# A four-layer network on one core: layers 1 and 2 with three images in flight, and the scan's first states moved from TensorE to ScalarE

## The reference

```
h_new = exp(dt * A) * h_prev + dt * B * x
y     = sum over the 16 states of h_new * C
```

## Time and profile before

| what | us |
|---|---|
| median of 3 runs | 5764.54 (5763.57 to 5771.34) |
| profiled execution, its own time | 5764.76 |
| its span, first to last instruction | 5763.0 |
| start to the first scan | 129 |
| layer 0 with its scans | 129 to 3424 |
| layer 1 of image 0 alone, with the end of layer 0 | 3424 to 3673.8 |
| rounds 0, 1, 2, 3 of layers 1 and 2 | 277.6, 300.6, 289.8, 131.6 |
| layer 3 | 4673.4 to 5763.0 |

### The profile page before, as it was taken

The page is one execution under the profiler, slowest core; times in us unless marked ns, Lnnn a source line. Parts: engine busy times, 40 slices in busy tenths (PEclk is TensorE's granted clock), DMA queues, the critical chain, the costliest instruction groups (busy, mean ns, idle before and its releaser), DMA issues. The chain is left out here.

```text
span 5763.0 us, 81471 instructions
## 1 busy us (share of the span) xinstructions
PE 5022.4 (87%) x30948; PEld 4080.8 (71%) x30948; DVE 4308.4 (75%) x4771; ACT 2958.0 (51%) x5242; POOL 2869.7 (50%) x3500
## 2 busy tenths in 40 slices
PE   4898999998989989999899877778878879999999
PEld 2776777776777767777777753565656669999998
DVE  1999999999999999999999986484847553333333
ACT  3766677766677766666666633131313223333332
POOL 3776777776776776777777634362535310000000
PEclk8999999999999999999999987788888889999999
DMA  2000000000000010000000011002020010010100
GB/s 72 1 16 27 9 9 9 9 23 20 9 9 9 16 31 13 9 9 9 9 9 9 5 40 60 20 25 74 25 74 13 28 54 25 25 34 25 34 25 21
DMA packets 88530, 136.93 MB, mean 24 GB/s; under 512 B 5284, under 2 KB 85184, under 8 KB 88140
## 3 DMA queue, kind: packets, MB, share of 16 engines
q1 hardware_dynamic: 88140, 131.72, 7.0%
HBM read 89.23 MB, written 42.47 MB: 23 GB/s over the span
## 5 line engine op out<-in xcount | busy, mean ns | idle before, releaser
L730 DVE TENSOR_TENSOR_SCAN a_h<-a_dA,pw 128x770 f32<-128x770 f32 x1152 | 2012.5, 1747 | 130.0 <-PE pw L448 128.8
L595 ACT ACTIVATE a_dA<-a_dt,a_Aneg 128x384 f32<-128x384 f32 x2304 | 1314.5, 607 | 185.6 <-DVE a_h L730 176.4
L869 POOL TENSOR_SCALAR a_dBT<-a_dtxT,a_BC 128x768 f32<-128x768 f32 x1152 | 1024.6, 906 | 448.6 <-PE pw L448 345.6
L458 PEld LDWEIGHTS pw<-g_ident,a_h 128*128 128x128 f32 x6912 | 796.2, 142 | 491.8 <-DVE a_acc L750 197.6
L458 PE MATMUL pw<-g_ident,a_h 128*128 128x128 f32 x6912 | 968.4, 277 | 157.7 <-DVE a_acc L750 121.6
L750 DVE SCALAR_TENSOR_TENSOR a_acc<-pw,a_BC,a_acc 128x768 f32<-128x768 f32 x960 | 960.7, 1001 | 84.3 <-PE pw L458 56.7
L447 PE MATMUL pw<-g_ident,a_dBT 128*128 128x128 f32 x6912 | 948.1, 274 | 4.8 <-POOL a_dBT L869 4.8
L447 PEld LDWEIGHTS pw<-g_ident,a_dBT 128*128 128x128 f32 x6912 | 795.5, 141 | 6.5 <-POOL a_dBT L869 5.4
L1829 DVE TENSOR_TENSOR d_hf<-d_hf,ps 128x384 f32<-128x384 f32 x288 | 159.0, 554 | 560.7 <-ACT d_hf L1759 553.5
L821 POOL TENSOR_TENSOR a_xin<-a_xin,a_tm 128x384 f32<-128x384 f32 x432 | 432.9, 1002 | 32.7 <-ACT a_tm L517 7.7
L406 PE MATMUL ps<-a_xn,a_WinT 128*128 128x384 f32 x864 | 365.6, 525 | 30.7 <-ACT a_sz L573 15.1
(11 more groups left out here) (243 smaller groups left out, 9666.0 us busy)
## 6 DMA issues: line engine op xcount, KB each, us to landing
b_xs<-x SPq DMA_DIRECT2D x36, 576.0 KB, 5.0
a_xs<-in_x SPq DMA_DIRECT2D x24, 576.0 KB, 3.9
x<-a_xs SPq DMA_DIRECT2D x24, 576.0 KB, 3.0
b_x<-x SPq DMA_DIRECT2D x24, 576.0 KB, 4.4
e_xs<-x SPq DMA_DIRECT2D x24, 576.0 KB, 3.9
out<-e_xs SPq DMA_DIRECT2D x24, 576.0 KB, 3.0
a_sx<-in_x SPq DMA_DIRECT2D x54, 192.0 KB, 2.4
x<-b_x SPq DMA_DIRECT2D x16, 576.0 KB, 3.1
```

Of the source, the lines that this page charges most:

```text
L458: t = e.transpose(m["pw2"][:, c * 128:(c + 1) * 128], m[f"a_h{g % 2}"][:, c, 1 + tb * 128:1 + (tb + 1) * 128], ident[:])
L595: e.activation(m[f"a_dA{idx // 2 % NDA}"][:, idx % 2, 1:T + 1], m[f"a_dt{k % 2}"][:, c, :], ACT.Exp, scale=m["a_Aneg"][:, c, n:n + 1]).the ...
L730: e.tensor_tensor_scan(m[f"a_h{g % 2}"][:, c:c + 2, :].rearrange("p c t -> p (c t)"), m[f"a_dA{pi % NDA}"][:].rearrange("p c t -> p (c t)" ...
L869: t = e.tensor_scalar(m[f"a_dBT{g % 2}"][:, tb, :], m[f"a_dtxT{o}"][:, tb, :], m[f"a_BC{o}"][:, tb, n:n + 1], 1.0, ALU.mult, ALU.mult)
```

## The change

**Layer 0, first states.** The small matmul L448 is gone. A pair's PSUM columns are laid out as 771 elements: a constant 0, group one, a constant 1, a constant 0, group two (the three constants are written once, at the start, by VectorE). Column 0 of `a_dA` holds the first state of group one, the column under the constant 1 holds a decay of 0, and the next holds the first state of group two; the scan starts from 1.0, so that 1.0 times the state plus 0 is the state. ScalarE copies the two states from `a_st` into `a_dA` with one small instruction behind each pair's second exponential. `pe_b` moves to the last transpose, GpSimd's `kept` waits for ScalarE (`a_exp`) where it waited for TensorE, and `a_exp` counts three per pair.

**Layer 0, lent sums.** `LENT` has 7 entries, with 26 and 43 added.

**Layers 1 and 2.** `mix` is split into tasks with due times of their own: tokens, each convolution part, gelu and gate, outputs. Ahead of round 0 stand the end of layer 0 (its due times scaled by 0.35, so that it runs in with the tokens of image 0), all of layer 1 of image 0, and for image 1 the tokens and convolution part 0. Round b then has the rest of image b+1 (parts 1 and 2, all outputs, `head`) and, for image b+2, statistics, tokens and part 0. `head` is due at units 32 to 53 where it was at 49 to 53. The banks of PSUM are dealt out anew: token images have one bank where they had two, the outputs, statistics and gate logits share one bank (`sums_bank`, under one `Turn`), and the pixels' two banks are used by nothing else. The image `b_ti` is written under waits for the part of the convolution that still reads it. The DMA queue loads the rows for image b+3's statistics in round b.

```
-LENT = (20, 22, 24, 38, 41)
+LENT = (20, 22, 24, 26, 38, 41, 43)
...
-        if q > 0:
-            w.wait_ge("p_st", g - NS + 1)
-        first = m["a_st"][:, c:c + 2, p // 3] if q > 0 else m["a_zero"][:]
         for h in range(2):
             for tb in range(TB):
-                at = COL + h * (T + 1) + 1 + tb * 128
-                e.transpose(ps[:, at:at + 128], ...)
-        e.matmul(ps[:, COL:COL + T + 2:T + 1], ident[:], first, start=True, stop=True, skip_group_check=True).then_inc(s["pe_b"], 1)
+                at = COL + 1 + h * (T + 2) + tb * 128
+                t = e.transpose(ps[:, at:at + 128], ...)
+        t.then_inc(s["pe_b"], 1)
...
+            if c % 2:
+                if k % NQ > 0:
+                    w.wait_ge("p_st", g - NS + 1)
+                w.wait_ge("p_const", 4)
+                e.activation(dA[:, 0:T + 3:T + 2], m["a_st"][:, c - 1:c + 1, n] if k % NQ > 0 else m["a_zero"][:], ACT.Copy).then_inc(s["a_exp"], 1)
...
-        w.wait_ge("a_exp", 2 * pi + 2)
+        w.wait_ge("a_exp", 3 * pi + 3)
+        e.tensor_tensor_scan(m[f"a_h{g % 2}"][:, p % 3, :], m[f"a_dA{pi % NDA}"][:], m[f"pw{pi % 2}"][:, COL:COL + PAIR], 1.0, ALU.mult, ALU.add)...
...
+def win_at(b, n):
+    if b == 0:
+        return 5 + 1.2 * n
+    if b == 1:
+        return 31 + 1.9 * min(n, 11) + 0.9 * max(0, n - 11)
+    return 4 + 2.4 * n
+def conv_at(b, g, k):
+    if b == 0:
+        return 18 + 11.2 * g + 1.2 * k
+    if g == 0:
+        return (52.5 if b == 1 else 44.5) + k
+    return 1.5 + 11.5 * (g - 1) + 1.15 * k
+def out_at(b, g, i):
+    at, gap = (((31, 0.9), (42.2, 0.9), (53.4, 0.5)) if b == 0 else ((7.8, 0.6), (14.2, 0.9), (25.8, 0.8)))[g]
+    return at + gap * i
...
+def held(g):
+    return (0, 1, 1, 2, 2, 2)[g]
...
 def l12_dve(e, m, w):
-    march([post_dve(e, m, w, NCH - 1), norm_dve(e, m, w, 0, 0)], 0)
-    march([mix_dve(e, m, w, 0), matrices_dve(e, m, w), norm_dve(e, m, w, 1, 30)], 0)
-    march([head_dve(e, m, w, 0)], 0)
+    march([early(post_dve(e, m, w, NCH - 1), POST), pieces_dve(e, m, w, 0, 0.1, 0.3), norm_dve(e, m, w, 0, 2.6), tokens_dve(e, m, w, 0), matrices_dve(e, m, w),
+           conv_dve(e, m, w, 0, 0), conv_dve(e, m, w, 0, 1), conv_dve(e, m, w, 0, 2), gated_dve(e, m, w, 0), outputs_dve(e, m, w, 0),
+           pieces_dve(e, m, w, 1, 24, 0.7), norm_dve(e, m, w, 1, 29.2), tokens_dve(e, m, w, 1), conv_dve(e, m, w, 1, 0), head_dve(e, m, w, 0, 57.2, 61),
+           pieces_dve(e, m, w, 2, 55, 1)], 0)
     for b in range(NB):
-        side = [tail_dve(e, m, w, b - 1)] if b > 0 else []
-        side += [mix_dve(e, m, w, b + 1), head_dve(e, m, w, b + 1)] if b + 1 < NB else [weights3_dve(e, m, w)]
+        side = [tail_dve(e, m, w, b - 1)] if b > 0 else []
         if b + 2 < NB:
-            side.append(norm_dve(e, m, w, b + 2, NORM_AT))
+            side += [norm_dve(e, m, w, b + 2, 2), tokens_dve(e, m, w, b + 2), conv_dve(e, m, w, b + 2, 0)]
+        if b + 3 < NB:
+            side.append(pieces_dve(e, m, w, b + 3, 42, 1.9))
+        if b + 1 < NB:
+            side += [conv_dve(e, m, w, b + 1, 1), conv_dve(e, m, w, b + 1, 2), gated_dve(e, m, w, b + 1), outputs_dve(e, m, w, b + 1),
+                     head_dve(e, m, w, b + 1, 32.2, 51.5)]
         march(side, UNITS, lambda u: sparse_dve(e, m, w, b, u))
```

More of the change, by code:

```diff
@@ L1174, in mix_act @@
         e.activation(m["b_feff"][:], F1[:, 0:C], ACT.Copy).then_inc(s["a_f"], 1)
[L1176 to L1178 removed]
+    for n in range(NT + 2):
+        if n < NT:
+            yield win_at(b, n) + 0.5
             u = NT * b + n
@@ L1213, in gelu @@
-    def gelu():
-        for g in range(3):
-            v = m[f"b_cv{g % 2}"]
-            yield out_at(g, 0) - 3.4
-            w.wait_ge("v_c", 54 * b + 18 * (g + 1))
-            e.activation(v[:, 0, :], v[:, 0, :], ACT.Gelu).then_inc(s["a_g"], 1)
-            yield out_at(g, 0) - 2.9
-            w.wait_ge("p_c2", 24 * b + 8 * (g + 1))
-            w.wait_ge("p_g", 3 * b + g + 1)
-            e.activation(v[64:128, 1, :], v[0:64, 2, :], ACT.Gelu).then_inc(s["a_g"], 1)
-    yield from woven(tokens(), image(), products(), gelu())
+            w.wait_ge("v_c", 54 * (b - 1) + 18 * (held(r) + 1))
@@ L1367, in woven, with tokens_dve @@
-def woven(*gens):
-    side = [Paced(g) for g in gens]
-    while any(p.at is not None for p in side):
-        at = min(p.at for p in side if p.at is not None)
-        yield at
-        for p in side:
-            if p.at is not None and p.at <= at:
-                p.at = next(p.gen, None)
-                break
+def tokens_dve(e, m, w, b):
+    for n in range(NT):
+        yield win_at(b, n + 1) + 0.6
+        u = NT * b + n
+        w.wait_ge("pe_fw", u + 1)
+        w.wait_ge("a_f", 1)
+        w.wait_ge("pe_iv", u - 1)
+        e.tensor_tensor(m[f"b_tf{u % 2}"][:], token_banks(m)[1][:, 0:C], m["b_feff"][:], ALU.mult).then_inc(m.s["v_tf"], 1)
@@ new lines, in gated_dve, with outputs_dve @@
+def gated_dve(e, m, w, b):
+    for g in range(3):
+        v = m[f"b_cv{(3 * b + g) % 2}"]
+        yield out_at(b, g, 0) - 2
+        w.wait_ge("a_g", 6 * b + 2 * g + 2)
+        e.tensor_tensor(v[64:128, 1, :], v[64:128, 1, :], v[64:128, 2, :], ALU.mult).then_inc(m.s["v_g1"], 1)
+def outputs_dve(e, m, w, b):
+    s, x = m.s, m[f"b_x{b % 2}"]
+    for i in range(NT):
+        r, o = divmod(i, 3)
+        yield out_at(b, *divmod(i, 6)) + 0.3
+        w.wait_ge("pe_wo", NT * b + i + 1)
+        w.wait_ge("p_na", NT * (b + 1))
+        w.wait_ge(f"d_x{b % 2}{r}", 16 * (b // 2 + 1))
+        e.tensor_tensor(x[:, o, rows(r)], x[:, o, rows(r)], sums_bank(m)[:, 0:T], ALU.add).then_inc(s["v_y"], 1)
+        yield out_at(b, *divmod(i, 6)) + 0.55
+        w.wait_ge("v_y", NT * b + i + 1)
+        w.wait_ge("pe_gn2", b)
+        e.bn_stats(m["b_bn1"][:, o, r, :], x[:, o, rows(r)]).then_inc(s["v_b2"], 1)
@@ L1530, in mix_pool @@
-    yield from woven(normal(), sums(), gated())
+    for r in range(NQ):
+        yield win_at(b, 0) - 0.8 if r == 0 else win_at(b, 3 * r - 2)
+        src, sem, value = strip(m, b, r, 1)
+        w.wait_ge(sem, value)
+        w.wait_ge("v_b1", GN * (b + 1))
+        w.wait_ge("pe_t1", NT * b + 3 * (r - 1))
+        for c in range(CT):
+            e.tensor_scalar(m[f"b_xa{r % 2}"][:, c, :].rearrange("p (j h w) -> p j h w", j=3, w=16), patches(src[:, c]),
+                            sc[:, 0, c:c + 1], sc[:, 1, c:c + 1], ALU.mult, ALU.add).then_inc(s["p_na"], 1)
```

482 lines of the change are left out of this document (244 added, 238 removed).

## The result

| | us |
|---|---|
| kernel after, median of 4 runs | 5616.18 (5612.2 to 5624.31) |
| kernel before, beside it, median of 4 | 5767.94 (5763.57 to 5776.34) |
| ratio | 0.9737, 95% interval 0.972 to 0.9754 |
| profiled execution after, its own time and its span | 5612.2, 5610.3 |

What follows compares the result with a forecast made beforehand. VectorE was taken to set the pace in layer 0, with no engine full in layers 1 and 2 except in pieces. 5764.8 us less 79 (layer 0) and 135 (layers 1 and 2) gave 5551 us, range 5440 to 5660.

Steps and rivals of the forecast that it cites:

- ten named waits at 0.22 ... I take 3.0 us a chunk: Layer 0, first states: less VectorE waiting for TensorE wins 3.0 us a chunk, ends 0 and 8.0.
- 5 x 0.2 = 1.0 us lost a chunk: Layer 0: about five ScalarE copies ahead of `a_ob` delay the others by 1.0 us a chunk, ends 0 and 3.0.
- rival C: Layer 0: TensorE idles more and its clock falls; 20% at the low level would cancel both gains, 214 us; chance 0.05.
- 1.3 us a chunk: Layer 0, two more lent sums: VectorE's relief of 1.8 us, less chain delays, wins 1.3 a chunk, ends 0.6 and 1.8.
- chunks of about 133 us: Layer 0: a sign that the forecast is right, chunks of about 133 us where one undisturbed chunk took 136.4.
- Ahead of round 0: Layers 1 and 2, first stage: 183 us of VectorE work at 75% fill takes 244 us, against 249.8 before.
- some 3 us: Outputs sharing one bank: TensorE's wait for VectorE's addition is covered at 0.6 to 0.9 units apart, some 3 us.
- Rounds 0 and 1: Layers 1 and 2: earlier `head` shortens the rounds' end, winning 20 us (to 258) and 25 us (to 276).
- Round 2: Layers 1 and 2: 53 us less for tokens, 25 for `head`, 7 for taps, so 205 us from 289.8.
- the 7 us credited for taps: Round 2: 7 us less for taps that nothing covers.
- A: Layer 0: ScalarE takes TensorE's place, giving 5630 us; sign, TensorE waits for `a_ob` or `a_tm` beyond 3 us a chunk; chance 0.13.
- B: Layers 1 and 2: VectorE and GpSimd collide, mean tap rises to 1.9 us, giving 5637 us; chance 0.14.

Runs made afterwards that it cites:

- e3: The changed kernel with the five lent sums of before (20, 22, 24, 38, 41), so without 26 and 43; 0.9741 of the kernel before.
- e6: The changed kernel with TensorE's x projection in layer 0 due later (48.3 + j instead of 47 + 1.2 j); 0.9704 of the kernel before.
- e5: The changed kernel with only lent sum 26 taken back; 0.9708 of the kernel before, 17 us less than the change.
- e8: The changed kernel with the later x projection, two output banks ahead of round 0, and lent sum 26 replaced by 35; 0.9656 of the kernel before.
- e9: The changed kernel with the later x projection, two output banks ahead of round 0, and six lent sums (no 26, no 35); 0.9654 of the kernel before.
- e11: The changed kernel leaving out 36 of 54 input matmuls of layer 1 for image 0 (incomplete computation); 0.9718 of the kernel before.
- e4: The changed kernel with image 0's outputs ahead of round 0 alternating between two PSUM banks; 0.9714 of the kernel before.
- e7: The changed kernel with `head` late again, at units 49 to 52; 0.9808 of the kernel before, 41 us more than the change.
- e1: The kernel before with only layer 0's part of the change, layers 1 and 2 as before; 0.9835, 5677.4 us.

## Why the prediction came out as it did

**Layer 0, first states: right in kind, too small.** The step "ten named waits at 0.22 ... I take 3.0 us a chunk" gave 5.0 (e3, in chunks that keep the clock, with the copies already in it). The named waits undercounted. Pairs 10 to 13 and 17 went from 2.83 to 2.60 us each, and most of pairs 37 to 44 by 0.1 to 0.4: wherever TensorE has a projection at its side, it set the period, and the 0.22 us of the earlier trace rows came back whole. Such pairs don't show as long waits, but as a period above the 1.66 + 0.91 us of the earlier trace rows.

**The copies ahead of `a_ob`: right place, half the delay, other mechanism.** "5 x 0.2 = 1.0 us lost a chunk" was drawn as plain delay. The term is too large, since a copy takes 0.09 us of ScalarE's queue and not 0.2: the wait for `a_ob` grew by 0.46 us, from 2.15 to 2.61. And the delay is not passed on. Pair 23 in a chunk that keeps its clock is 4.09 us, where it was 4.19: nothing is lost. The cost comes through rival C in miniature: in ten of the 19 chunks with this wait the clock falls, 1.65 us each (132.95 against 131.3), 17 us in all. e6 takes it away. That the longer wait is what brings the falls is borne out by the counts (none in 19 chunks at 2.15 us in the kernel before, 7 to 16 in 19 at 2.61 us in each of seven runs, none in the 19 at 0.4 us in e6); why one chunk falls and the next does not is open.

**Two lent sums: the sum failed.** "1.3 us a chunk" was 0.2 (131.3 against e3's 131.4): 43 gives its 0.87 in full, and 26 loses 0.7 (e5), because its product stands in ScalarE's queue behind the softplus pieces. The prediction had named that place and still priced it positive. 35 lost 0.5 us a chunk in e8 (130.7 against e9's 130.2).

**The chunk of 133 us: luck.** The prediction's sign "chunks of about 133 us" came true in the ten chunks that lose the clock. Most of the others take 131.3: the states gave more than their term, the lent sums less, and what brings the chunk back to 133 is a fall of the clock that the forecast had not summed.

**Ahead of round 0: the step that failed most, 244 forecast, 273.** It divided all of VectorE's work by a fill of 75%. VectorE's busy time was forecast at 183 us and is 169 (8 us of this because the 64 taps took 1330 ns in the mean, not 1457), which by the same division would be 19 us less; the fill was 62%. The 68.7 us ahead of the first convolution hold 23.0 us of VectorE's work; at 75% these would take 31 us, so 38 us are missing from the forecast. There the end of layer 0 and the tokens of image 0 run through TensorE, and little for VectorE is ready (e11). The 204.4 us behind them have a fill of 71%, which is another 10 us over 75%, and the single output bank cost 12 us there (e4). 38 + 10 - 19 are the 29 us by which 273 passes 244. The prediction had this wait as what could eat the gain and put it down as covered at "some 3 us" between outputs; with taps of 1 to 2.6 us in front of the addition it is not.

**Rounds 0 and 1: mis-sized, 20 and 25 forecast, 8 and 13 measured.** (Round 0 of the order before varies from 273.9 to 279.9 us, so its 8 may be 5 to 10.) "What they win is the end" is right, and e7 gives 10 and 12 for it. The mistake was to take GpSimd's 28.9 and 15.4 us as time that all would win. The freed stretch fills with taps moved there until VectorE is full.

**Round 2: 205 forecast, 227.** 14 of the 22 us are the same step (25 credited for `head`, e7 gives 11; over the three rounds 70 were credited and 33 came, so it alone is some 37 us). The rest I can't assign, and the 7 us credited for taps stood on no row: this round takes 227 or, more often, 234 us by its clock, and the profiled run of the change is one of the short ones.

**Rivals.** A is refuted as a whole (the chunk did fall by 3.5 to 5.1 us), but it holds for 26 and 35, and its sign did show: TensorE's waits for `a_ob` and `a_tm` in chunk 10 went from 2.1 to 3.6 us, past the 3 that the prediction set. B is refuted: mean taps fell. C came in ten pieces of 3.4 us, not in 20% of the stage. The forecast held because its range was wide. The errors had two signs, 17 us too little for layer 0 and 73 too much for layers 1 and 2; without the 17 the time would be 5633 us, still in the range and faster, but at the price that stands for A. So the total alone does not tell the stories apart; the stages do.

**A better version.** e8 and e9 take 5570 us, 0.9655 of before and about 47 us less than the change. They keep it, drop 26, and add the second output bank and the later projection.

## What to carry to other kernels

Price a relief of an engine by periods, not by named waits: count the steps whose period lies above the bound's own cadence and has that engine's side work in it. Never apply one fill to a stage whose work isn't ready at its start; cut it where the first piece of the bounding engine's work can begin. Before work is lent to a helping engine, look at what is due in its queue in the next two steps: a lent sum won 0.87 us in a quiet place and lost 0.5 or 0.7 us in a busy one. Price a small instruction by the step to the next one's start and not by its length. And before an edit is given the credit for a few us in a stage, see how far that stage varies among runs in which its instructions are the same.

## What the runs showed of the hardware that was not expected

- A wait of TensorE of 2.6 us, recurring in 19 of 24 chunks, was followed by a piece at 1.2 GHz in 10 of them (16, 16, 8 and 8 in the profiled runs of e1, e4, e7 and e11, whose layer 0 has the same instructions; 13 in e3, 7 in e5). With the wait at 2.15 us, in the kernel before, and at 0.4 us, in e6, it was in none.
- The same six units of round 2 ran in 27.0 or 32.4 us with the clock at 0.87 or 0.68, while everything ahead of them in the round was alike within 0.1 us. Why the clock parts there is open.
- A ScalarE copy of two columns takes 193 ns (187 to 213 over 960 of them), of 96 columns 236. The instruction behind it starts 94 ns after it, so that it costs ScalarE's queue half of its length.
- The scan of 771 elements in one instruction takes 1751 ns in the mean, that of 770 took 1747.
